# Graph network over dense adjacency: every event of a graph on its own step, one subtraction from GpSimd to VectorE

## What is computed

```python
# layer 0: attention, 4 heads of 16; h = x, a = adj
feats   = einsum('bnf,hfo->bhno', h, kernel)
scores  = einsum('hbnd,hbdm->hbnm', f_self, f_other)     # f_self, f_other: h times two weights
masked  = a * scores
masked  = where(masked >= 0, masked, 0.2 * masked) / sqrt(16) + where(a == 0, -1e9, 0)
attn    = softmax(masked) * (a != 0)
x = layernorm(x + relu(einsum('bhnm,bhmo->bhno', attn, feats) + bias))
# layer 1: mean over neighbours and the node once more
A = a + eye(N);  x = layernorm(x + (A @ x) / sum(A, axis=2))
# layer 2: x = layernorm(x + (adj @ (x @ W) + b))
# layer 3: t = adj @ x;  x = layernorm(x + where(t > 0.5, 1, 0))
def layernorm(x, eps=1e-5): return (x - mean(x)) / sqrt(var(x) + eps)
```

## Time and profile before

| | us |
|---|---|
| median of 3 runs | 1550.73 |
| lowest, highest | 1539.59, 1557.88 |
| the profiled execution | 1557.14, its span 1555.3 |

### The profile page before, as it was taken

One profiled execution on the slowest core, in us unless ns is written; L12 is line 12 of the kernel. 1 busy time (PEld: TensorE's weight loads), 2 busy tenths in 40 slices (PEclk: granted clock), 3 DMA queues, 4 the chain that ended last, 5 costly groups with the idle time before them and its releaser, 6 DMA issues.

```text
span 1555.3 us, 20985 instructions
## 1 busy us (share of the span) xinstructions
PE 1374.7 (88%) x7296; PEld 692.2 (45%) x7296; DVE 1243.9 (80%) x1498; ACT 1223.9 (79%) x1404; POOL 1053.2 (68%) x562
## 2 busy tenths in 40 slices
PE   4798898998989999998999989899999989799766
PEld 2343444554444444444444544444444444345323
DVE  2779899778888778778897888888788888977764
ACT  1599898887878878788888878888788888878641
POOL 3177777767778766787677786777667876866412
PEclk9889899899999999999999999999999999989968
DMA  6734453243433433333343344335333433100000
...
DMA packets 140879, 84.95 MB, mean 55 GB/s; under 512 B 100372, under 2 KB 130522, under 8 KB 140762
## 3 DMA queue, kind: packets, MB, share of 16 engines
...
...
## 4 chain that ended last, share of the span: by engine, by line
PE 50%; POOL 12%; ACT 12%; issue 12%; DVE 11%; DMA 2%; SPq 1%; ACTq 0%; POOLq 0%; DVEq 0%
PE M L603 10%; PE Z L569 10%; PE M L658 9%; PE Z L576 8%; POOL LS L502 8%; ACT LS L750 6%; PE Z L587 4%; ACT LS L758 4%; PE Z L672 3%; PE Z L612 3%; DVE LS L912 3%; DVE RP L898 2%; POOL RSTD L507 2%; DMA adj_cast<-in_adj_dram 1%; PE Z L726 1%
## 5 line engine op out<-in xcount | busy, mean ns | idle before, releaser
L502 POOL TENSOR_TENSOR LS<-LS,MB 125x1000 f32<-125x1000 f32 x372 | 867.1, 2349 | 354.3 <-DVE LS L912 290.4
L750 ACT ACTIVATE LS<-Z 126x1000 f32<-126x1000 f32 x576 | 575.5, 1000 | 168.5 <-PE Z L576 167.3
L898 DVE TENSOR_TENSOR RP<-LS,RP 125x1000 f32<-125x1000 f32 x480 | 575.5, 1199 | 86.0 <-ACT LS L750 65.0
L758 ACT ACTIVATE LS<-LS 125x1000 f32<-125x1000 f32 x576 | 596.4, 1036 | 45.8 <-POOL LS L502 26.8
L569 PE MATMUL Z<-AT,BI 126*126 126x500 fp8e4 x1152 | 381.2, 414 | 78.0 <-ACT LS L750 50.4
L576 PE MATMUL Z<-FS,FO 128*125 128x500 f16 x1152 | 361.5, 396 | 0.0
L603 PE MATMUL M<-LS,V 126*18 126x500 f32 x2304 | 323.9, 637 | 3.9 <-ACT LS L758 3.8
L569 PEld LDWEIGHTS Z<-AT,BI 126*126 126x126 bf16 x1152 | 128.8, 143 | 391.3 <-ACT LS L750 183.0
L912 DVE TENSOR_TENSOR LS<-LS,MB 125x1000 f32<-125x1000 f32 x204 | 286.3, 1408 | 5.0
L576 PEld LDWEIGHTS Z<-FS,FO 128*125 128x125 f16 x1152 | 167.7, 146 | 99.1 <-issue 20.4
L658 PE MATMUL M<-AT,XP 125*128 125x500 fp8e4 x756 | 195.3, 381 | 0.0
...
## 6 DMA issues: line engine op xcount, KB each, us to landing
MB<-row_maxima SPq DMA_DIRECT2D x48, 500.0 KB, 4.0
...
```

What stands on the lines that cost most here:

```text
L502: nc.gpsimd.tensor_tensor(rows, rows, MB[:P, u % 2, :, :], ALU.subtract).then_inc(sub_pool, 1)
L750: nc.scalar.activation(LS[:PD, q % RL, :, :], banks("Z", q)[:PD], ACT.Prelu, alpha=SLOPE).then_inc(bent, 1)
L758: nc.scalar.activation(rows, rows, ACT.Exp, scale=0.25).then_inc(exps, 1)
L898: nc.vector.tensor_tensor(run, rows, run, ALU.max).then_inc(maxed, 1)
```

## The change

- The steps of all events now stand in tables, one number each. The events of the layers move: the power one step sooner in its table (POOL's subtractions too, by one), the nine parts of `collect` one step sooner in layers 0 to 2, the copies with them; `turn_back` and `add_up` stay. The features go from 16, 17, 20, 21, 23, 25, 27, 28, 32 to 15, 16, 18, 19, 20, 23, 26, 28, 31. POOL's loads of the third slice (numbered 2) go from 62, 64, 66, 68 to 58, 60, 61, 65, and those of the next graph's first from 27, 29, 31, 33 to 29, 31, 30, 33.
- `low` of layers 0 to 2 goes from POOL to DVE (`low_rows`).
- The counts: of each count's two columns DVE takes one and adds 1 in the same instruction; the addition over all counts (L952) goes.
- Order within a step. ACT: `high` and `take` now stand ahead of the bend, and `take` is one step later. DVE: `centre` stands ahead of `row_maxima`; in layer 1 `add_squares` stands behind the subtraction. PE: the turned maxima stand last in their step.
- SP: the spread maxima from one step after the turn to three, the transposes from 3, 15, 47 to 7, 16, 49, the next x from 10 to 8, the finished rows from 13 to 10, XA from 29 to 26.
- The subtractions of the last steps, which DVE takes alone, begin one step later.

```diff
-LAG = 18
-SUB_AT = LAG + 0
-EXP_AT = LAG + 2
-WEIGH_AT = LAG + 4
...
-RT_AT = STEPS + MAX_AT + 1
-TAKE_AT = STEPS - 1 + WEIGH_AT + 0
...
+POOL_AT, SUB_AT, EXP_AT, WEIGH_AT = 17, 18, 20, 22
+LAG = POOL_AT
+TURNED = (14, 14, 14, 14, 14, 14)
+SPREAD = (17, 17, 17, 17, 17, 17)
+TAKE = (34, 34, 34, 34, 34, 34)
...
+POWER = (27, 44, 63, 81)
+COLLECT = ((33, 34, 35, 36, 37, 38, 39, 40, 41),
...
+FEATURES = (15, 16, 18, 19, 20, 23, 26, 28, 31)
...
+TRANSPOSES = (7, 16, 49)
+XF_AT, STORE_AT, XA_AT = 8, 10, 26
...
@@ SP @@
-                if turned_at(q - 1) is not None:
-                    spread_maxima(turned_at(q - 1))
+                u = turned_at(q, SPREAD, LAST_RT + 1)
+                if u is not None:
+                    spread_maxima(u)
@@ POOL @@
-            def low(b, l):
-                pool.wait_ge(xh_ready, 3 * b + l + 1)
-                nc.gpsimd.tensor_tensor(XP[:, :, F:2 * F], X[:, :, :], XP[:, :, 0:F], ALU.subtract).then_inc(xp_ready, 1)
...
+                if layer_at(q, POWER):
+                    power(*layer_at(q, POWER))
                 if load_at(q) and load_at(q)[0] >= NS:
                     load(*load_at(q))
...
-                e = q - LAG
+                e = q - POOL_AT
@@ ACT @@
-                if q < QN and q % GROUP == 0:
-                    for n in range(GROUP):
-                        bend(q + n)
...
+                if layer_at(q, HIGH):
+                    high(*layer_at(q, HIGH))
+                if unit_at(q, TAKE) is not None:
+                    take(unit_at(q, TAKE))
+                if q < QN:
+                    bend(q)
@@ DVE @@
-                    nc.vector.tensor_reduce(DEG[:, s * ST:(s + 1) * ST], sums[:, :, :, D + 1], AX.X, ALU.add)
+                    nc.vector.tensor_scalar(DEG[:, s * ST:(s + 1) * ST], sums[:, :, 0, D + 1], 1.0, None, ALU.add)
...
+            def low_rows(b, l):
+                dve.wait_ge(xh_ready, 3 * b + l + 1)
+                nc.vector.tensor_tensor(XP[:, :, F:2 * F], X[:, :, :], XP[:, :, 0:F], ALU.subtract).then_inc(xp_ready, 1)
...
-            def neighbours(b, n):
-
-                if n == 0:
-                    dve.wait_ge(kept_seq, 5 * (UPG * b + NS))
-                    nc.vector.tensor_scalar(DEG[:, :], DEG[:, :], 1.0, None, ALU.add).then_inc(den_seq, 1)
-                    return
-                dve.wait_ge(den_seq, 2 * b + n)
+            def neighbours(b):
+
+                dve.wait_ge(kept_seq, KEEPS * (UPG * b + NS))
                 nc.vector.reciprocal(RDEN[:, :], DEG[:, :]).then_inc(den_seq, 1)
```

224 lines of the change are left out of this document (115 added, 109 removed).

## The result

| | median, us | lowest, highest | ratio to before | 95% interval |
|---|---|---|---|---|
| before | 1550.16 | 1539.59, 1557.88 | | |
| changed | 1583.57 | 1576.66, 1586.47 | 1.0205 | 1.0171 to 1.0240 |

A forecast was written before the change was run, and what follows sets the result against it. No one engine was taken to bound a whole graph; the lead passes between them. Gains -38, late MB +15 and start +5 make -18 us on 1557.1 profiled; from the median 1550.7 this gives 1532 us, range 1505 to 1560.

The forecast's parts named there:

- The gains, 38 us: Layers 0 and 2, last copies, less 0.3 for layer 1: 5.4 us a graph saved, 38 in seven graphs.
- layer 0: Steps 26 to 35: earlier centre, `low` off POOL, first part of `collect` under a wait; 2.7 us a graph saved.
- Layer 2, 2.6 us: Steps 63 to 70: load and `low` leave POOL's path, `collect` moves under the wait; 2.6 us a graph saved.
- `low_rows` at 0.95 us: On DVE, 21 at 0.95 us each, priced at 0; the skill's lockout would make them 20 to 56 us.
- The first graph, 5 us: At the start, later row of ones (3.9 us) and transposes ahead of the first spread (1 to 3): together 5 us lost.
- The late MB, 15 us in six graphs: Spread row maxima queue late on SP, so ACT waits at step 20: 2.5 us a graph, 15 in six graphs.
- the 1 us for a slower clock: Behind PE's idle at the late MB: may take 1 us, against 1 that POOL's and DVE's catching up may give back.
- (d): Rival: late MB at its upper price, 6 us a graph, 36 in all; 1573 us; 12 in 100.
- (b): Rival: MB's delay at step 20 is not felt; 1517 us, 1503 to 1524; 28 in 100.
- (c): Rival: time won at layers 0 and 2 is waited for in the next collecting stretch; 1554 us; 18 in 100.
- The signs: Waits expected ahead of `high`, in layer 2, at SP's spread (6 us), ACT's exponential 0 (2 to 3), PE's ones (11).
- neither sign of being wrong: Wrong if ACT doesn't wait at step 20, or if the collecting stretches grow by what the layers gave.

The follow-up runs named there:

- the base: Changed kernel with all of SP's steps as before (spread 15; transposes 3, 15, 47; next x 10; finished rows 13; XA 29): 1510.05 us.
- e7: The base with `high` and `take` behind the bend of their step again on ACT: 1528.18 us.
- e12: The base with the sum of the squares and the scale ahead of all else of their steps on VectorE: 1550.00 us.
- e16: Kernel before with only `low` of layers 0 to 2 moved from POOL to VectorE, behind the row maxima: 1530.71 us.
- e6: The base with `low` of layers 0 to 2 on POOL again, ahead of its subtraction: 1544.66 us.
- e10: Changed kernel with the spread at 15 and transposes at 3, 15, 47; next x, finished rows and XA stay as changed: 1520.27 us.
- e1: Changed kernel with the row maxima spread at step 15 again, ahead of the six transposes, not at 17: 1526.04 us.

## Why the prediction was wrong, point by point

- **The gains, 38 us: right in sum, in part by luck.** The base shows some 40. By place (table above; the profiled runs differ by 7.5 us a graph, somewhat more than the medians do) layer 0 gave 3.2 us against my 2.7, layer 2 only 0.6 against 2.6, and layer 1 with its step 47 gave 1.4 where I had a loss of 0.3. Another 2.0 came at steps 9 to 13, where I had nothing and where the clock is low in the kernel before and mostly not in the base. So 3.4 of the 7.5 us are nothing that I foresaw, and without them the gain would be 4.1 us a graph against my 5.4. At layer 0 X did come 1.1 us sooner behind bend 26, as I had it (10.67 against 11.73); ACT's wait for the centre fell from 2.81 to 0.20 us, and a wait of 2.1 us stands ahead of `high` (below), as the text had it. Bend 26 to bend 36 takes 25.0 us in the base and 23.8 in the changed kernel, against 26.8 before: 1.8 and 3.0 against my 2.7.

```profile
939.08 0.84 ACT L805 ACTIVATE XP<-Y 125x768 f32<-125x768 f32 x1 [0.20 <-DVE Y L968]
...
947.93 0.84 ACT L809 ACTIVATE XP<-X 125x768 f16<-125x768 f32 x1 [2.08 <-DVE X L985]
...
1038.27 0.64 PE L576 MATMUL Z<-AT,BI 126*126 126x500 fp8e4 x2 [2.50 <-ACT LS L751]
```

- **Layer 2, 2.6 us: over-sized.** PE's gap of 3.12 us became 2.50 and 0.69. Step 62 to 70 gave 1.1 us in the mean of five graphs of the base, and 0.6 are left of it by step 9 of the next graph. PE's clock is low at 67 to 69 behind the gap in each of these graphs; I had set nothing for it. That `high` ahead of the bend makes this gap is not shown: with it behind the bend again (e7) the gap is 2.73 us.
- **`low_rows` at 0.95 us: mis-sized, harmless.** It took 1078, 2225 and 2242 ns (shortest, median, longest), 40.7 us in all 21, between my 20 and 56. The scale with as many elements is 0.95 us in all its 28 instances. The rule of the Trainium skill that I set against this move (SBUF — State Buffer, two separate sides) is borne out: the 14 long instances have a POOL instruction beside them all the time, the 7 short ones for 0.3 to 0.6 us, and in e12, where seven have none beside them at all, these take 0.95. DVE hid it: e16 and e6 show the move worth 21 to 35 us.
- **The first graph, 5 us: right for the wrong pair.** Start and first two graphs together lost 5.1 us against before (37.8, 157.2 and 175.0 against 36.8, 152.5 and 175.8), but 16 against the base (149.0 and 167.6), which has the gains as well. The ones were issued at 57.79, 1.6 us later than my 56.2, and landed 9.3 us behind their issue, not 3.4 as before: PE waited 17.3 us and not near 11. I had moved the issue and kept the landing. And this wait was not the loss: e10 takes 12 us of it away, and its first graph is as long as e1's.

```profile
57.79 0.74 SPq L382 DMA_DIRECT2D AT<-ONE  x1
...
67.16 1.09 PE L576 MATMUL Z<-AT,BI 126*126 126x500 fp8e4 x2 [17.29 <-DMA AT<-ONE]
```

- **The late MB, 15 us in six graphs: the step that failed.** Changed kernel against base, these graphs differ by 62 us, 10.4 each. The place, the queue and the order of the waits were as predicted. From the end of the last scale to the first exponential I had 22.4 us (945.97 to 968.4); it took 25.1. The four FO issues took 4.34 us and not 2.43, right behind the store (about 1.9), and the first subtraction, beside DVE's own (979.79, ahead of POOL's by 0.05), 3.3 and not 2.3. So ACT waited 5.0 us and not 2.0: what is left of a long delay behind slack takes the whole error of the delay. Then steps 20 and 21 are 6.3 us longer than in the base, step 23 by 3.4, step 11 by 1.2. For the last two my sum had nothing: the 1 us for a slower clock was set off against 1 us of catching up. So the path was right, and its price failed: 2.5 us a graph by the sum, 10.4 measured. The term also left out what the other moves of SP cost: e10 against the base has 10 us, and e1 against e10 about 6, where I had only the start's 5.
- **The rivals.** (d), the late MB at its upper price, was the right mechanism with 12 in 100. It put the threshold at 5 us a graph and the price at 6; the price is 10.4. (b) is refuted by e1, and (c) in sum by the base, though at layer 2 it comes near.
- **The signs.** Each place that I named for a wait had it, and neither sign of being wrong came. What was off was every size on SP's side: the spread 8.2 us behind its reduction and not 6, ACT's wait 5.0 and not 2 to 3, PE's wait for the ones 17.3 and not 11.
